# A token pipeline with attention over heads: score matmuls in four parts of the array, queries laid out by four tokens, and another order on PE, ACT and DVE

## The reference

```python
cq = h_t @ Wc + bc
q = concat(cq @ Wcq + bcq, rope(cq @ Wqr + bqr))      # per head 32 + 16
ckv = h_t @ Wckv + bckv
k = concat(ckv @ Wck + bck, rope(h_t @ Wkr + bkr))
v = ckv @ Wv + bv
scores = einsum('bsid,bsjd->bsij', q, k) * SCALER     # i, j: 16 heads
out = einsum('bsij,bsjd->bsid', softmax(scores), v) @ Wo + bo
```

## Time and profile before

| | |
|---|---|
| runs, median (lowest to highest) | 2026.46 us (2020.72 to 2035.89), 3 runs |
| profiled execution, its time | 2029.77 us |
| its span, first to last instruction | 2027.8 us |
| mean granted TensorE clock | 0.975 |
| busy PE / DVE / ACT / POOL | 1893.7 / 1520.7 / 1091.5 / 550.1 us |
| token pipeline | up to about 1400 us of the span |

### The profile page before, as it was taken

One profiled execution on the slowest core, in us unless ns is written; L12 is line 12 of the kernel. 1 busy time (PEld: TensorE's weight loads), 2 busy tenths in 40 slices (PEclk: granted clock), 3 DMA queues, 4 the chain that ended last, 5 costly groups with the idle time before them and its releaser, 6 DMA issues. The chain is left out here.

```text
span 2027.8 us, 49115 instructions
## 1 busy us (share of the span) xinstructions
PE 1893.7 (93%) x14529; PEld 1504.8 (74%) x14529; DVE 1520.7 (75%) x3935; ACT 1091.5 (54%) x1745; POOL 550.1 (27%) x773
## 2 busy tenths in 40 slices
PE   5899999999999999999999999985899999988886
PEld 4788888888888888888888888874454555546664
DVE  6588888888888888888888888773444444429997
ACT  4576767666666767666666767651222233223333
POOL 1111112111111112111111111110344444427776
PEclk8799999999999999999999999997899999999998
DMA  5245454545454454545455554437999999979994
GB/s 189 69 129 147 128 153 129 151 128 150 124 143 138 133 150 128 150 129 152 126 140 137 137 146 128 140 108 222 334 299 284 274 310 307 291 202 394 406 398 171
DMA packets 414103, 383.99 MB, mean 189 GB/s; under 512 B 289704, under 2 KB 298024, under 8 KB 413992
## 3 DMA queue, kind: packets, MB, share of 16 engines
q1 hardware_dynamic: 393504, 324.98, 53.1%
q0 software_dynamic: 14336, 35.66, 7.5%
q10 hardware_dynamic: 6208, 22.68, 2.9%
HBM read 232.46 MB, written 150.63 MB: 189 GB/s over the span
## 5 line engine op out<-in xcount | busy, mean ns | idle before, releaser
L861 POOL TENSOR_SCALAR ve<-mv 128x1 f32<-128x1 f32 x192 | 42.7, 222 | 1073.1 <-DVE mv L698 1072.3
L593 ACT COPY qT<-bank 48x512 f32<-48x512 f32 x256 | 269.1, 1051 | 72.2 <-PE bank L445 67.6
L593 ACT COPY kT<-bank 48x512 f32<-48x512 f32 x256 | 268.8, 1050 | 4.8
L1068 PE MATMUL e_gu<-w,xgT 128*128 128x384 f32 x512 | 184.3, 503 | 15.4 <-DMA w<-w_ed 13.5
L452 PE MATMUL bank<-wgu,xfT 128*128 128x416 f32 x512 | 189.1, 369 | 8.3 <-ACT xfT L593 8.3
L453 PE MATMUL bank<-wgu,xfT 128*128 128x416 f32 x512 | 183.5, 358 | 0.0
L642 ACT ACTIVATE prob<-prob 128x512 f32<-128x512 f32 x128 | 78.7, 633 | 176.3 <-DVE prob L795 176.3
L469 PEld LDWEIGHTS score_ps<-kT,qT 48*64 48x64 f32 x4096 | 133.4, 138 | 40.7 <-issue 40.7
L469 PE MATMUL score_ps<-kT,qT 48*64 48x64 f32 x4096 | 151.1, 225 | 11.5 <-ACT kT L593 11.5
L1068 PEld LDWEIGHTS e_gu<-w,xgT 128*128 128x128 f32 x512 | 93.2, 192 | 74.7 <-DMA w<-w_ed 14.2
L1229 DVE SCALAR_TENSOR_TENSOR tanh<-tanh,e_gu 128x192 f32<-128x192 f32 x64 | 22.7, 354 | 166.3 <-ACT tanh L1155 166.3
(11 more groups left out here) (177 smaller groups left out, 4922.8 us busy)
## 6 DMA issues: line engine op xcount, KB each, us to landing
w<-w_eg SPq DMA_DIRECT2D x60, 768.0 KB, 6.7
acc_scratch<-zero SPq DMA_DIRECT2D x130, 256.0 KB, 4.2
w<-w_ed SPq DMA_DIRECT2D x60, 384.0 KB, 11.0
xf_scratch<-xf SPq DMA_DIRECT2D x64, 288.0 KB, 2.1
xin<-x SPq DMA_DIRECT2D x64, 256.0 KB, 2.9
v_scratch<-v SPq DMA_DIRECT2D x64, 256.0 KB, 3.7
vbd<-v_scratch SPq DMA_DIRECT2D x128, 128.0 KB, 3.2
o_scratch<-o SPq DMA_DIRECT2D x256, 64.0 KB, 2.3
```

Source lines behind the costliest of these rows:

```text
L593: nc.scalar.copy(dst, src).then_inc(done.sem, 1)
L1068: last = nc.tensor.matmul(gu_ps[par], xgT[:, par, n, :], w1[:, place, n, :], start=(n == 0), stop=(n == KD - 1))
```

## The change

- `qT` and `kT` take 2 x 48 partitions: tokens of every other four go to partitions 0 to 47 and 64 to 111. In qT four tokens of one head now lie side by side (head, token), in kT each token's heads lie as before. `spread` so makes four copies for each former two, of 256 elements.
- `scores` issues all 32 matmuls of a tile together, in turn on four parts of the array (two row halves r and two column halves g).
- As the rows of the scores are now (head, token), the mask constant and the layout of `o_scratch` change; `oin` is loaded in four DMAs of 32 partitions each (tokens n, n + 4, ...), with two settling no-operations on SP ahead.
- On PE the scores stand between the halves of the gate/up product; q's products (wq) come before the first half; the third part of wlat behind k's transposes; the transposes of xn before those of prob; rank behind pv.
- ACT copies the first half of kT ahead of xfT; the second tanh stands behind oT, the routing exponential behind latT.
- DVE has the softmax behind the first gated half, q's sums ahead of it, the second gated half and the routing behind it, xT's low part behind the row sum, and yn at the very end.

```diff
-    c[:, C_NEG:C_NEG + B4] = np.where((p[:, None] // H) % B4 == np.arange(B4), 0.0, -BIG)
+    c[:, C_NEG:C_NEG + B4] = np.where(p[:, None] % B4 == np.arange(B4), 0.0, -BIG)
...
-    o_d = nc.dram_tensor("o_scratch", (2, P, D), F32).ap()
+    o_d = nc.dram_tensor("o_scratch", (2, P // B4, B4 * D), F32).ap()
...
-        qT, kT = qT_all[0:DQ], kT_all[0:DQ]
+        qT = qT_all[:, 0:P // 2, :].rearrange("p (c x) y -> p c (x y)", x=B4).rearrange("p c (h t) -> p c h t", t=B4)
+        kT = kT_all[:, 0:P // 2, :]
...
-        o_in = count("o_in", 16)
+        o_in = count("o_in", 64)
...
                     sp.wait_ge(o_in.sem, o_in.at(i - 5))
-                    dst = o_d[1 - par].rearrange("(c g b t) (h d) -> g b (t h) c d", c=8, g=2, b=2, h=H)
+                    dst = o_d[1 - par].rearrange("(c g b) (x d) -> g b x c d", c=8, g=2, b=2, d=DH)
                     src = o[:].rearrange("p (c b d) -> p b c d", c=8, b=2)
                     for g in range(2):
                         for b in range(2):
                             sp.dma_start(dst[g, b], src[64 * g:64 * g + 64, b]).then_inc(o_out.sem, 16)
                     sp.wait_ge(o_out.sem, o_out.at(i - 3))
+                    settle(sp)
                     sp.wait_ge(pe_oT.sem, pe_oT.at(i - 4))
-                    sp.dma_start(oin[:], o_d[1 - par]).then_inc(o_in.sem, 16)
+                    settle(sp)
+                    src = o_d[1 - par].rearrange("c (h t d) -> t c h d", t=B4, d=DH)
+                    for n in range(B4):
+                        sp.dma_start(oin[n:P:B4, :].rearrange("p (h d) -> p h d", d=DH), src[n]).then_inc(o_in.sem, 16)
...
 
-            def scores(blocks):
-
-                for blk in blocks:
-                    for g in range(2):
-                        t0 = (blk // 2) * 16 + g * 8 + (blk % 2) * B4
-                        last = nc.tensor.matmul(score_ps[64 * g:64 * g + 64, blk * 64:blk * 64 + 64],
-                                                qT[:, t0:t0 + B4, :].rearrange("p t h -> p (t h)"),
-                                                kT[:, t0:t0 + B4, :].rearrange("p t h -> p (t h)"),
+            def scores():
+
+                for blk in range(NBLK // 2):
+                    four = (blk // 2) * 4 + blk % 2
+                    for g, r in ((0, 0), (1, 1), (1, 0), (0, 1)):
+                        c4 = four + 2 * g
+                        part = slice(64 * r, 64 * r + DQ)
+                        at = r * 512 + blk * 64
+                        last = nc.tensor.matmul(score_ps[64 * g:64 * g + 64, at:at + 64],
+                                                qT[part, c4].rearrange("p h t -> p (h t)"),
+                                                kT[part, B4 * c4:B4 * c4 + B4, :].rearrange("p t h -> p (t h)"),
...
-                    product(b5, [xT[:, :, n, :] for n in range(KD)], [wlat[:, :, n, :] for n in range(KD)], d_xT, i, pe_lat)
+                    high(*latents)
...
+                if active(i):
+                    pe.wait_ge(d_xT.sem, d_xT.at(i))
+                    low(*latents, pe_lat)
...
+                    pe.wait_ge(a_rank.sem, a_rank.at(i - 6))
+                    settle(pe)
+                    scores().then_inc(pe_s.sem, 1)
+                if active(i - 3):
+                    pe.wait_ge(o_in.sem, o_in.at(i - 3))
+                    pe.wait_ge(a_kT.sem, a_kT.at(i - 2, 4))
+                    transposes(b3, [oin[:, n * P:(n + 1) * P] for n in range(KD)], pe_oT)
+                if active(i - 5):
+                    pe.wait_ge(d_q.sem, d_q.at(i - 1, 1))
+                    pe.wait_ge(d_pv.sem, d_pv.at(i - 3))
+                    product(b4[:, 0:GU], normed, [wgu[:, :, n, GU:] for n in range(KD)], d_xfT, i - 5, pe_gu)
...
                 def spread(dst, src, done, n):
 
-                    dv = dst.rearrange("p t (m a) -> p a m t", a=2)
                     for a in range(2):
-                        copy(dv[:, a, 4 * n:4 * n + 4, :],
-                             src[64 * a:64 * a + DQ, :].rearrange("p (m t) -> p m t", t=P), done)
+                        sv = src[64 * a:64 * a + DQ, :].rearrange("p (m r c t) -> p r m c t", m=4, r=2, t=B4)
+                        for r in range(2):
+                            copy(dst[64 * r:64 * r + DQ, a, 4 * n:4 * n + 4], sv[:, r], done)
...
-                    spread(qT, b3, a_qT, 0)
+                    by_four = qT.rearrange("p c (m a) t -> p a m c t", a=2)
+                    spread(by_four, b3, a_qT, 0)
                     act.wait_ge(pe_qT.sem, pe_qT.at(i - 2, 2))
-                    spread(qT, b7, a_qT, 1)
+                    spread(by_four, b7, a_qT, 1)
+                if active(i - 2):
+                    act.wait_ge(pe_kT.sem, pe_kT.at(i - 2, 1))
+                    by_token = kT.rearrange("p (c t) (m a) -> p a m c t", t=B4, a=2)
+                    spread(by_token, b3, a_kT, 0)
...
-                    act.wait_ge(pe_kT.sem, pe_kT.at(i - 2, 1))
-                    spread(kT, b3, a_kT, 0)
                     act.wait_ge(pe_kT.sem, pe_kT.at(i - 2, 2))
-                    spread(kT, b2, a_kT, 1)
```

More of the change, by code:

```diff
@@ L286, in token_pipeline @@
         a_latT = count("a_latT")
-        a_qT = count("a_qT", 4)
-        a_kT = count("a_kT", 4)
+        a_qT = count("a_qT", 8)
+        a_kT = count("a_kT", 8)
         a_exp = count("a_exp", 2)
@@ L462, in turn, with high, low @@
                                  for m in range(4 * n, 4 * n + 4)], done)
-            def scores(blocks):
-                for blk in blocks:
-                    for g in range(2):
-                        t0 = (blk // 2) * 16 + g * 8 + (blk % 2) * B4
-                        last = nc.tensor.matmul(score_ps[64 * g:64 * g + 64, blk * 64:blk * 64 + 64],
-                                                qT[:, t0:t0 + B4, :].rearrange("p t h -> p (t h)"),
-                                                kT[:, t0:t0 + B4, :].rearrange("p t h -> p (t h)"),
+            def scores():
[8 more added lines that the diff above has]
+                                                kT[part, B4 * c4:B4 * c4 + B4, :].rearrange("p t h -> p (t h)"),
                                                 start=True, stop=True)
                 return last
+            def high(dst, lhs, rhs):
+                for n, (a, b) in enumerate(zip(lhs, rhs)):
+                    nc.tensor.matmul(dst, a[:, 0], b[:, 0], start=(n == 0), stop=False)
+                    nc.tensor.matmul(dst, a[:, 0], b[:, 1], start=False, stop=False)
+            def low(dst, lhs, rhs, done):
+                for n, (a, b) in enumerate(zip(lhs, rhs)):
+                    last = nc.tensor.matmul(dst, a[:, 1], b[:, 0], start=False, stop=(n == len(lhs) - 1))
+                last.then_inc(done.sem, 1)
             def iteration(i, par):
+                latents = b5, [xT[:, :, n, :] for n in range(KD)], [wlat[:, :, n, :] for n in range(KD)]
+                normed = [xfT[:, :, n, :] for n in range(KD)]
                 if active(i - 2):
@@ L548, in iteration @@
                     transposes(b3, [lat[:, n * P:(n + 1) * P] for n in range(2)], pe_latT)
+                if active(i + 1):
+                    pe.wait_ge(d_ln[0].sem, d_ln[0].at(i + 1))
+                    pe.wait_ge(a_kT.sem, a_kT.at(i - 2))
+                    transposes(b2, [xn[:, n * P:(n + 1) * P] for n in range(KD)], pe_xT)
                 if active(i - 2):
@@ L557, in iteration @@
                     product(b6, [latT[:, 1 - par, :, 1, :]], [wck[:, :, 0, :]], d_latT, i - 1, pe_k)
-                if active(i + 1):
-                    pe.wait_ge(d_ln[0].sem, d_ln[0].at(i + 1))
-                    pe.wait_ge(a_kT.sem, a_kT.at(i - 2, 4))
-                    transposes(b2, [xn[:, n * P:(n + 1) * P] for n in range(KD)], pe_xT)
-                if active(i - 5):
-                    pe.wait_ge(d_r.sem, d_r.at(i - 5, 7))
-                    pe.wait_ge(a_pT.sem, a_pT.at(i - 2))
-                    nc.tensor.matmul(rank_ps, chosen[:], tri[:], start=True, stop=True).then_inc(pe_rank.sem, 1)
                 if active(i - 2):
@@ L755, in iteration @@
                                             ALU.add).then_inc(d_lat.sem, 1)
+                if active(i):
+                    dve.wait_ge(pe_lat.sem, pe_lat.at(i))
+                    dve.wait_ge(pe_latT.sem, pe_latT.at(i - 1))
+                    nc.vector.tensor_tensor(lat[:], b5[:, 0:2 * DC], blat[:, 0:2 * DC], ALU.add).then_inc(d_lat.sem, 1)
+                if active(i + 1):
+                    dve.wait_ge(pe_xT.sem, pe_xT.at(i))
+                    normalise(0, xn[:], xin[:, 1 - par, :], i + 1)
+                if active(i - 5):
+                    dve.wait_ge(a_xfT.sem, a_xfT.at(i - 5))
+                    low_part(xfT, s0, d_xfT)
                 if active(i - 1):
```

163 lines of the change are left out of this document (74 added, 89 removed).

## The result

| | before | after |
|---|---|---|
| median (lowest to highest), 20 runs each | 2029.49 us (2018.38 to 2037.91) | 2043.33 us (2026.64 to 2051.39) |
| profiled execution, its time | 2029.77 us | 2050.91 us |
| its span | 2027.8 us | 2048.9 us |

The ratio is 1.007, with a 95% interval from 1.005 to 1.009: slower, by less than the 1% that the prediction counts as a difference. The forecast was 2053 us (1990 to 2095). The profiled execution of after lies 7.6 us above its median, so differences between the two traces are somewhat larger than those between the medians.

What follows compares the result with a forecast made beforehand. TensorE's own work bounded the kernel at 20.7 us a tile; the loop through oin would take over at 21.2. Steady +30 us, filling -6, draining +3: net +27, forecast 2053 us (1990 to 2095).

Steps and rivals of the forecast that it cites:

- the loop through oin: Once per tile through PE, DVE, SP's writes of o and load of oin: from 20.03 us to 21.2, setting the period.
- From PE's transposes to k's sum: Loop stretch from PE's transposes of oin through wck to k's sum on DVE: 8.28 us against 7.82, +0.46.
- From the fourth load to the transposes: Loop's end, from the last load of oin on SP to PE's transposes: landing 2.3 us, plus 0.27 for PE's start.
- Filling: First three tiles, where PE waits for kT: copied 0.8 us sooner, some -2 us each, -6 us.
- The drain: Last tiles, as the pipeline empties: oin later by 1.8 us in two tiles, +3 us.
- forecast: Likeliest case: the loop through oin sets a period of 21.0 to 21.4 us a tile, 2053 us; chance 0.42.
- level: Rival: same loop, each term 0.1 to 0.2 us smaller, 20.8 us a tile, about 2030 us; chance 0.25.
- The step that took half of the possible gain: Scores on PE in four parts: of a possible 1.08 us out of 2.16 per tile, 0.55 gained.
- The rival in which ScalarE becomes the bound: If qT's copies take 0.61 us too, the loop through PE is 22.1 us, about 2107 us; chance 0.08.
- xf's scale: On DVE between k's sum and o: with yn behind o it runs without GpSimd's x1 beside it, 0.6 us less.
- Issue is cheap: Rival: four loads of oin 0.34 us apart, settling free; PE's 20.15 us sets the period, about 1988 us; chance 0.18.
- slow landing: Rival: oin lands as slowly as vbd, 3.2 us; 22.1 us a tile, about 2105 us; chance 0.07.

Runs made afterwards that it cites:

- One load: Changed kernel with oin loaded by one DMA of whole rows, rows left in another order so output is not the reference's: 1995.28 us, ratio 0.982.
- DVE's doses in both directions: Changed kernel with yn put back ahead of o (2094.03 us), xT's low part moved behind o (2016.50), or k's sum moved there too (2002.65).
- yn back: Changed kernel with yn on DVE behind k's sum and ahead of o again, instead of behind o: 2094.03 us, ratio 1.030.
- each half of the change alone: Kernel before with only the new layout, loads and four-part scores: 2135.30 us; changed kernel with those as before, only the new order: 2102.80 us.
- o first: Changed kernel with k's sum and xT's low part moved behind o on DVE: 2002.65 us, ratio 0.985.
- layout alone: Kernel before with the new qT, kT, mask, o_scratch, four loads, settling instructions and four-part scores, in the old order: 2135.30 us, ratio 1.048.

## Why the prediction was right, and where it was not

**What bounds it.** Right: the loop through oin, which had 0.4 to 0.7 us to spare, became the bound, with PE waiting at the transposes of oin in nearly every tile, 0.68 us for about 1 forecast. One load, and DVE's doses in both directions, show it. A period near 21.2 was forecast; 21.00 came in the middle of the run and 20.85 over all steady tiles.

**Terms of the loop.** From PE's transposes to k's sum 8.02 us for 8.28 forecast: the step from the transposes to the next product takes 0.41, not the 0.58 that it took before a group of scores, and the 0.07 for a change of weights does not appear. DVE to o's end 3.66 for 3.81. First write to first load 4.29 for 4.44: the two settling instructions cost 0.10 together, not 0.25. Loads 0.65 apart, for 0.66. From the fourth load to the transposes 3.1, for 2.57 (2.3 of landing and 0.27): this is the term that was mis-sized against the change, since I scaled it from the wait for the last write; the transfer of vbd, the other one that reads DRAM in 128-byte pieces, was nearer. The sum is right to 0.2 us, as three terms were 0.1 to 0.3 too large and one 0.5 too small.

**Sum.** The profiled executions differ by 21 us for 27 forecast, and this is nearer than its terms. The period cost 8 us over 53 tiles in place of 30 over 59. Filling gave back 5.5 us up to the third o, for 6 forecast, but then lost 7.3 again in the next four periods, which the prediction had at nothing: there the loop already made PE wait, once for 3.55 us with the clock falling behind it. The drain cost some 10, for 3. The medians differ by 13.8 us where I said 27. So the sign and the mechanism held and the size was half: by the bound of 1% this is the case "within 1%", to which the prediction gave 0.3, and it lies between "forecast" and "level".

**Scores.** The step that took half of the possible gain was too low. 64 records take 1.10 us where they took 2.16, the full factor of two (1.06 us a tile gained, for 0.55). It made no difference to the time, as the loop stood over it. What did enter PE's own need and was not foreseen are the waits for probT and xfT, 0.66 a tile: need 20.22 in the run with one load, for 20.15 forecast, which is luck: a gain 0.51 larger and waits of 0.66 nearly cancel. The cause of the larger one is an edit that I had called "only moved": the transposes of xn had covered ScalarE's copy of probT, and ahead of prob's transposes they cover nothing. The prediction checked when the exponentials are late, but not what stands behind the transposes of prob.

**Copies.** As worked out: qT 367 ns and kT 603 ns a copy, for 370 and 610 (the page, by mean):

```profile
L615 ACT COPY kT<-bank 48x256 f32<-48x256 f32 x512 | 308.7, 603 | 11.0
...
L615 ACT COPY qT<-bank 48x256 f32<-48x256 f32 x512 | 187.8, 367 | 33.8 <-PE bank L450 22.9
```

The rival in which ScalarE becomes the bound falls with the 367. qT is written four f32 at a time and costs what dense data do; by the Trainium skill ("SBUF — State Buffer", the note on cachelines in The DMA port swizzle) consecutive accesses to the same 16-byte line run at full bandwidth, which is four f32, and these rows agree.

**xf's scale.** Right in size, half right in cause. All 64 take 0.25 us:

```profile
L856 DVE TENSOR_SCALAR xf<-ex,erec x64: 254/254/258, 116.0 to 1431.0; 128x64 f32<-128x64 f32 x64
```

I put this down to yn's move behind o. With yn back it takes 0.25 us too: by the rows of both orders what matters is whether xf starts within GpSimd's x1, and moving xT's low part is enough to bring it ahead of x1.

**Rivals.** "Issue is cheap" falls with the 0.65 between loads; "slow landing" was half true (3.1 from the last issue to PE, where it would have been 3.5).

## What to carry to other kernels

Where two bounds lie within half a microsecond of each other, price every edit on both: here each half of the change alone cost 1.2 to 1.6 us a tile, and together 0.15 to 0.3, and of a gain of 1.06 us on the engine that was busy all the time 0.74 were worth little or nothing until a DVE instruction or two had been moved behind the one that feeds the round trip through DRAM. In such a loop put first, on each engine, what the next link waits for; that alone turned +0.7% into -1.5% with the same layout. When an instruction is "only moved", ask what it covered where it stood. And look at a period in more than one stretch: the one from 400 to 1000 us had twice the loss of the whole.

## What the hardware did that I had not expected

- The 32 score matmuls (two records each) take 1.10 us in four parts, read in "o first", where nothing is waited for behind them: 34 ns a matmul, 17 ns a record. In two parts, with one row half at a time, it is 1.84 us, 29 ns a record, faster than the 34 ns of the old layout. The Trainium skill ("TensorE: Matmul & The Clock Gate", Back-to-back issue gap) has a floor of about 25 ns from start to start. I had applied it to the records, and there it does not hold in these rows; per matmul they do not contradict it.

```profile
711.66 1.16 PE L477 MATMUL score_ps<-kT,qT 48*64 48x64 f32 x64
712.76 0.66 PE L450 MATMUL bank<-c,oin 128*128 128x128 f32 x4
```

- Four loads of 32 partitions in a row: 0.65 us between starts, and 3.1 us from the last start to PE, no sooner than behind the one load before (2.97), though each carries a quarter of it.
- xf's scale, 64 elements a partition, takes 254 ns when it begins 0.22 us ahead of GpSimd's x1, and a median of 896 in the kernel before, where it starts behind x1's start. The row sum, which ran beside x1 with yn back, kept its 1.21 us.
- The granted clock can fall in the middle of a busy stretch. Behind the wait of 1.56 us at 571.68 in the changed kernel the granted clock is 0.50, and each of the four falls in that stretch of "yn back" stands behind a wait for oin of 1.49 to 1.88. Not every such wait brings one: in "layout alone", where most waits for oin lie between 1.2 and 2.8 us, 11 of 26 periods have a fall.
